# A fused cross-attention and Fourier feed-forward kernel: the adds of the output bias moved to other slots of GpSimd's program

## The reference, cut to what matters

```python
def attn(y, ctx, mask):                       # y = layernorm(x); 16 heads of 32
    q, k, v = y @ wq + bq, ctx @ wk + bk, ctx @ wv + bv
    score = (q k^T / sqrt(32)) * mask
    score = where(score == 0, -1e9, score)
    return softmax(score) v @ wo + bo
x = x + attn(layernorm(x), ctx_1024, mask)    # x: (2, 2048, 512) f32, ctx: (2, 128, 512)
x = x + real(ifft(fft(layernorm(x)) @ w)) + bias
```

## Time and profile before

| | us |
|---|---|
| median of 3 runs (461.54, 461.7, 462.95) | 461.7 |
| the profiled execution | 463.93 |
| its span, first to last instruction | 462.1 |
| PE / DVE / ACT / POOL busy | 442.5 / 397.6 / 373.4 / 365.0 |
| PE share of the chain that ended last | 78% |

### The profile page before, as it was taken

How to read it: one execution, slowest core, us unless ns; L and a number is a source line. 1 busy time by engine, 2 the same in 40 slices (tenths; PEclk the granted TensorE clock), 3 DMA queues, 4 the chain that set the end, 5 groups by cost and what they waited for, 6 DMA issues and landing times.

```text
span 462.1 us, 11172 instructions
## 1 busy us (share of the span) xinstructions
PE 442.5 (96%) x3510; PEld 292.7 (63%) x3510; DVE 397.6 (86%) x630; ACT 373.4 (81%) x1434; POOL 365.0 (79%) x544
## 2 busy tenths in 40 slices
PE   6989898998999999999999999999999999989997
PEld 4777676676666666666666666666666665545444
DVE  3797699899999999999999999999998899969443
ACT  3358588889999999898989898989899888969720
POOL 6598844797989898998979898989798666866663
PEclk9999999999999999999999999999999999989999
DMA  8996663322344554544565445454433344421244
GB/s 280 391 365 180 229 198 71 101 79 76 81 119 124 124 144 117 138 119 129 128 141 128 121 105 158 91 164 93 121 85 93 71 73 103 84 59 23 70 105 123
DMA packets 85287, 60.16 MB, mean 130 GB/s; under 512 B 40141, under 2 KB 72813, under 8 KB 84718
## 3 DMA queue, kind: packets, MB, share of 16 engines
q1 hardware_dynamic: 84508, 59.29, 47.3%
q10 hardware_dynamic: 722, 0.17, 0.2%
HBM read 29.33 MB, written 8.39 MB: 82 GB/s over the span
## 4 chain that ended last, share of the span: by engine, by line
PE 78%; DVE 9%; issue 4%; DMA 3%; SPq 2%; POOL 2%; ACT 1%; ACTq 1%; DVEq 0%; POOLq 0%
PE bank L438 33%; PE bank L525 17%; PE bank L582 10%; PE bank L599 7%; PE scores L570 5%; PE bank L443 3%; PE bank L595 3%; DVE zs L860 3%; SPq L276 2%; DMA xs<-in_x 1%; DVE zs L867 1%; DMA bqb<-in_bq 1%; DVE nmin L872 1%; PE scores L443 1%; POOL cl L1104 1%
## 5 line engine op out<-in xcount | busy, mean ns | idle before, releaser
L688 ACT ACTIVATE zs<-zs,nbias 128x128 f32<-128x128 f32 x512 | 199.9, 399 | 5.0 <-POOL nbias L1093 4.9
L688 ACT ACTIVATION_READ_ACCUMULATOR zs<-zs,nbias 128x1 f32 x512 | 100.4, 196 | 0.0
L867 DVE SCALAR_TENSOR_TENSOR zs<-zs 128x1024 f32<-128x1024 f32 x64 | 80.6, 1260 | 2.2
L860 DVE TENSOR_TENSOR zs<-scores,ms 128x1024 f32<-128x1024 f32 x64 | 78.0, 1218 | 0.3 <-issue 0.3
L872 DVE TENSOR_REDUCE nmin<-zs 128x8 f32<-128x1024 f32 x64 | 77.4, 1209 | 0.1
L525 PE MATMUL bank<-xth,wqh 128*128 128x256 f16 x256 | 70.3, 275 | 2.7 <-DVE kl L810 2.0
L697 ACT COPY pt<-bank 128x512 f32<-128x512 f32 x128 | 68.6, 588 | 4.8 <-PE bank L582 4.3
L525 PE MATMUL bank<-xtl,wqh 128*128 128x256 f16 x256 | 69.8, 273 | 0.0
L525 PE MATMUL bank<-xth,wql 128*128 128x256 f16 x256 | 69.8, 273 | 0.0
L582 PE MATMUL bank<-ident,zs 128*128 128x128 f32 x512 | 67.0, 274 | 0.0
L1053 POOL TENSOR_TENSOR xs<-xs,bob 128x256 f32<-128x256 f32 (+1 forms) x45 | 45.1, 1005 | 19.7 <-DVE zs L867 19.7
(11 more groups left out here) (118 smaller groups left out, 972.3 us busy)
## 6 DMA issues: line engine op xcount, KB each, us to landing
xs<-in_x SPq DMA_DIRECT2D x16, 512.0 KB, 4.1
xtr<-in_xt SPq DMA_DIRECT2D x16, 512.0 KB, 4.5
out<-x SPq DMA_DIRECT2D x31, 256.0 KB, 2.5
qs<-qh SPq DMA_DIRECT2D x120, 64.0 KB
lp<-in_lparts SPq DMA_DIRECT2D x4, 1024.0 KB, 9.7
qs<-ql SPq DMA_DIRECT2D x60, 64.0 KB
ms<-in_mask SPq DMA_DIRECT2D x16, 128.0 KB, 2.8
wqs<-in_wq SPq DMA_DIRECT2D x2, 512.0 KB, 7.0
```

The costliest lines, as they stand in the source:

```text
L688: last = act.activation(z, z, ACT.Exp, bias=nbias[:, s % 4, i:i + 1], scale=-NEG, accum_out=zsum[:, s % 4, i:i + 1])
L860: dve.tensor_tensor(zs[:, s % NZ], A[:].rearrange("p t (h k) -> p t h k", h=4), ms[:, c % NM].unsqueeze(2).broadcast_to([128, 2, 4, KEYS]) ...
L867: dve.scalar_tensor_tensor(out=z, in0=z, scalar=0.0, in1=z, op0=ALU.is_equal, op1=ALU.subtract).then_inc(eq_done, 1)
```

## The change

The slots of the adds are set by `bo_slot`. Chunks 3 to 12 are added four slots later than before, and chunks 13, 14 and 15 in slots 53, 55 and 57, where it was 51, 55 and 59. From chunk 12 on the tile 1 is no longer added in two halves but whole, in the slot after that of tile 0, and ahead of `bias(v)`.

| chunk | before: tile 0, left, right half of tile 1 | after |
|---|---|---|
| 3 ... 11 | 4c - 1, 4c - 1, 4c + 2 | 4c + 3, 4c + 3, 4c + 6 |
| 12 | 47, 47, 50 | tile 0 in 51, tile 1 in 52 |
| 13 | 51, 51, 54 | 53, 54 |
| 14 | 55, 55, 58 | 55, 56 |
| 15 | 59, 59, 62 | 57, 58 |

```diff
 def bo_slot(c):
-    return c + 7 if c < 3 else 4 * c - 1
+    return c + 7 if c < 3 else 4 * c + 3 if c < 13 else 2 * c + 27
...
                 for a in range(3, NC):
                     if bo_slot(a) == v:
                         add_bo(a, 0)
+                    if bo_slot(a) + 1 == v and a >= 12:
+                        add_bo(a, 1)
                 if 0 <= v < NS:
                     bias(v)
...
-                for a in range(3, NC):
+                for a in range(3, 12):
                     if bo_slot(a) == v:
                         add_bo(a, 1, slice(0, D // 2), False)
                     if bo_slot(a) + 3 == v:
                         add_bo(a, 1, slice(D // 2, D))
```

## The result

| | before | after |
|---|---|---|
| median of 20 runs | 463.22 us | 460.69 us |
| lowest, highest | 461.54, 465.31 | 460.30, 463.62 |
| profiled execution, its span | 463.93, 462.1 | 462.53, 460.7 |

The ratio of the times is 0.9959 (95% interval 0.9946 to 0.9972): 0.41% faster, 1.9 us. The medians lie 2.5 us apart, more than that, because the kernel before has two levels of time and its median falls into the upper one. The median of the three runs shown ahead of the prediction, 461.7, belongs to the lower level.

What follows compares the result with a forecast made beforehand. TensorE was taken as the bound until slot 56, then GpSimd's late `cl` before WO(13,0), with the clock falling. Gains 0.65 + 1.70 = 2.35 us off the 461.7 median gave 459.4, range 458.2 to 462.0.

Steps and rivals of the forecast that it cites:

- (a): Slots 11 to 47: chunks 3 to 11 moved four slots later, claimed to be worth 0.
- (b): Slots 51 to 54: moved adds fit GpSimd idle or are hidden by ScalarE's wait, claimed value 0.
- (c): Slots 55 and 56: one half leaves, a full add fits an idle of 3.07 us, claimed value 0.
- (d): Slot 57: added (15,0) delays nbias(57) by 1.25 us, `cl` is held, 0.6 us of new TensorE idle.
- (e): Slot 58: added (15,1) pushes x1nl into slot 59's compare, costing VectorE about 0.99 us.
- longest overlap of 0.25 us: Claimed longest overlap of a running GpSimd instruction with a VectorE compare in the trace of before.
- (f): Slot 59 loses its adds: `cl` ends earlier, WO(13,0) starts 0.65 us earlier; bounds 0 and 1.6.
- (g): TensorE clock at WO(13,0): with its 2.18 us stop split, it stays at 2.4 GHz, gaining 1.70 us; bounds 0 and 1.70.
- (h): Slot 62 loses its half add, but WO(14,0) still waits behind nbias(63): value 0, upper bound 0.65 us.
- taken off it, 459.4: Last step: the summed gain subtracted from the 461.7 us median of the runs, giving the forecast time 459.4.
- The sum of 2.35: Whole gain forecast, 0.65 from WO(13,0) starting earlier plus 1.70 from the clock, taking the profiled execution from 463.9 to 461.6.
- rival (1): The clock falls all the same or timed runs never paid for it: 0.65 alone, 461.0 us; chance 0.20.

Runs made afterwards that it cites:

- Experiment 2: Changed kernel with chunks 3 to 11 back in their old slots, only chunks 12 to 15 moved; 461.14 us, ratio 0.9960 to the kernel before.
- experiment 6: Chunks 3 to 12 as before, 13 in slots 51 and 52, 14 in 53 and 54, 15 in 60 and 61; 460.31 us, ratio 0.9945 to the kernel before.
- experiment 7: Kernel before with only chunk 15 moved, whole, to slots 60 and 61; 460.14 us, ratio 0.9947.
- experiment 8: Changed kernel with chunk 15 in slots 59 and 60, slots 57 and 58 empty; 460.21 us, ratio 0.9941 to the kernel before.
- experiment 9: Kernel before with tile 1 of chunk 14 added whole in slot 56, slot 59 keeping its full add; 460.15 us, ratio 0.9953.
- experiment 4: Kernel before with 2 matmuls, or 1 small one, in front or amid TensorE's stop before WO(13,0); ratios 0.9983, 0.9983 (2 matmuls), 1.0003, 0.9991 (1 small).
- experiment 3: Kernel before with 8 extra matmuls of 512 columns ahead of WO(13,0)'s wait for `cl`; 461.70 us, ratio 0.9976.

## Why the prediction was right or wrong, point by point

**What bounds the kernel; terms (a), (b), (c).** Right in the main. Experiment 2 shows the early part at nothing, and WO(13,0) and the clock there were the place. Term (c) was not quite 0: by the add in slot 56 the compare of slot 57 took 0.12 longer (experiment 6).

**Term (d), the add in slot 57.** Right in kind, too large. It put nbias(57) 1.25 late; it started 0.89 late, counted from slot 56 (10.35 for 9.46). Exponentials 0.39 late, not 0.75. The forecast had `cl` of slot 53 held, by a margin of 0.13 us; it was not held, as GpSimd was 0.34 us ahead of the forecast. Of that 0.28 stood already at the mask scaling of slot 56: there nbias(56) had started 0.07 earlier and the instruction after it 0.20 behind it instead of 0.41. So the mask scaling began 0.09 before the compare of slot 57 here (392.03 and 392.12) and not inside it, and the compare took 1.35. The rzb copy behind `cl` was held instead. New idle of TensorE 0.28, not 0.6, and it waited for VectorE's `cn`, later by the two long compares (0.12 and 0.15), a path that the forecast did not have.

**Term (e).** The mechanism was right: x1nl ran into the compare of slot 59 and the compare paid. The overlap was 0.42 and cost 0.28 (1.50 for 1.22), the same overlap less 0.14 as in the row it was worked out from. The forecast had an overlap of 1.13, since its GpSimd was later. The prediction's "longest overlap of 0.25 us" was a misreading: in the trace of before GpSimd's adds of `lp` ran until 31.06, 0.79 into a compare, and it took 1.86 for 1.22, the overlap less 0.15:

```profile
28.56 2.50 POOL L1118 TENSOR_TENSOR lp<-lp 128x512 f32<-128x512 f32 x2
...
30.27 1.86 DVE L867 SCALAR_TENSOR_TENSOR zs<-zs 128x1024 f32<-128x1024 f32 x1
```

The SBUF — State Buffer page of the Trainium skill (section "SBUF: two separate sides") has an exclusive lock, held for the whole instruction by whoever starts first. The traces agree up to these 0.79 us, with a loss 0.14 to 0.15 smaller than the overlap; no compare in any trace took more than 1.87, so a loss of a whole instruction is not shown.

**Term (f).** 0.65 forecast, 1.07 measured, inside the bounds of 0 and 1.6. Experiments 7, 8 and 9 came near the upper bound: 1.44 to 1.51.

**Term (g), the clock.** In the profiled execution it was 1.69 for a forecast of 1.70. The ground was wrong: not the one long stop but the idle around it counts (experiment 4). The change reduced that idle too, from 0.29 + 2.18 to 0.28 + 0.40 + 0.62, 1.17 us less, and in experiment 4 a stop 0.44 us shorter (1.74 for 2.18) was enough. The rule that the prediction named from TensorE: Matmul & The Clock Gate (Part 1) in the Trainium skill, that the slow clock is the default and recent activity lifts it, agrees with experiments 3 and 4: with 2 or 8 matmuls added the clock stayed up in 35 of 35 runs.

**Term (h).** Right: WO(14,0) comes 20.68 us after WO(13,0) in the changed kernel, 20.69 in the kernel before at full clock.

**The step that failed** is the last one, "taken off it, 459.4". The sum of 2.35 was made against one profiled execution, in which the clock had fallen, and was taken whole off a median of three runs, two of which (461.54 and 461.7), by their times, had no fall to give back. For those the sum is term (f) alone, and 461.7 less the measured 1.07 is 460.6, the level that the changed kernel has. The clock's 1.70 was there to be gained in about half of the runs, but it was not in the 461.7 from which it was taken. Taken off the median of 20 runs, 463.22, the same sum would have given 460.87 for the measured 460.69, which is partly luck, as term (f) was 0.42 too small. The warning was in the text: rival (1) said that the timed runs may never have paid for the clock, had the profiled time standing 2.2 us above the median for it, and gave 461.0; with 0.20 it was held too low. Over many runs of both kernels the gains are 1.0 at full clock and about 0.8 in the mean from fewer falls (53 of 91 times 1.8, less 2 of 20 times the 2.4 that those two lie above the rest), together 1.8 for the 1.9 measured.

## What to carry to other kernels

A profile is one execution. If its time stands apart from the median by as much as a term of the sum, see first whether the timed runs contain that term. Where GpSimd comes late to a deadline, look for any one instruction ahead of the deadline that can go to a slot with idle: one of two was enough here, and the smallest edit (chunk 15 alone) started WO(13,0) earlier than the whole change did. Put no new add in a slot in which the queue already runs without a gap.

## What the runs showed of the hardware that I had not expected

Adding two matmuls (0.43 us) to a stop of 2.18 us made the kernel faster, 0.9983 (0.9969 to 0.9997), since the slow clock that followed the stop in 53 of 91 runs followed in none of 24. The same program with the same stop goes either way from run to run: 461.7 or 463.4.

Which of two colliding instructions pays, GpSimd's or VectorE's compare, hung on a tenth or two of a us. The mask scaling of slot 56 (two instructions) began 0.18 us behind the compare of slot 57 in the trace of before, and the compare took its 1.23:

```profile
390.75 1.23 DVE L867 SCALAR_TENSOR_TENSOR zs<-zs 128x1024 f32<-128x1024 f32 x1
...
390.93 1.73 POOL L1086 TENSOR_SCALAR ms<-ms,rs 128x128 f32<-128x128 f32 x2
```

With an add in slot 56 it began 0.09 us ahead of the compare, and made it 0.12 us longer.
